# An audio tower on one core: fp16 terms for the mixture bias, causal attention with stationary values, and new order strings for every engine

## The reference, cut to what matters

```python
o = jnp.einsum('enh,ehd->end', h, W2) + b2[:, None, :]
y = jnp.einsum('ne,end->nd', comb, o)
...
scores = jnp.einsum('bhqd,bhkd->bhqk', q, k) * dh ** (-0.5)
causal = jnp.tril(jnp.ones((n, n), bool))
scores = jnp.where(causal, scores, jnp.finfo(scores.dtype).min)
attn = jax.nn.softmax(scores, axis=-1)
o = jnp.einsum('bhqk,bhkd->bhqd', attn, v)
y = o.transpose(0, 2, 1, 3).reshape(b, n, d) @ Wo
gate = jax.nn.softmax(y @ gate_W + gate_b, axis=-1)
...
out = jnp.einsum('bned,bne->bnd', eo, gate)
```

## Time and profile before

| | |
|---|---|
| median of 3 runs | 4183.73 us (4181.23 to 4189.27) |
| the profiled execution | 4183.28 us |
| its span, first to last instruction | 4181.6 us |
| busy share of the span | PE 96%, DVE 78%, ACT 66%, POOL 61% |
| granted clock of TensorE, mean | 0.984 of full speed |
| one round of the 30 | 122.3 us |

### The profile page before, as it was taken

How to read it: one execution, slowest core, us unless ns; L and a number is a source line. 1 busy time by engine, 2 the same in 40 slices (tenths; PEclk the granted TensorE clock), 3 DMA queues, 4 the chain that set the end, 5 groups by cost and what they waited for, 6 DMA issues and landing times.

```text
span 4181.6 us, 104776 instructions
## 1 busy us (share of the span) xinstructions
PE 3994.9 (96%) x41344; PEld 3003.6 (72%) x41344; DVE 3258.6 (78%) x8879; ACT 2767.7 (66%) x4797; POOL 2531.2 (61%) x2494
## 2 busy tenths in 40 slices
PE   9589999999999999999999999999999999999988
PEld 4256777777777777777777777777777777777766
DVE  4367887878888777888878888878878887887866
ACT  4236776766767666677776767776676777667654
POOL 2136666666666666666666666666666666666656
PEclk9679999999999999999999999999999999999999
DMA  6100100010110000111000011100111110010100
GB/s 184 40 28 29 31 27 23 16 31 29 31 31 27 21 20 29 31 31 31 19 22 26 29 31 31 31 19 18 30 29 31 31 31 19 17 31 29 29 16 7
DMA packets 137083, 127.62 MB, mean 31 GB/s; under 512 B 28944, under 2 KB 135376, under 8 KB 136592
## 3 DMA queue, kind: packets, MB, share of 16 engines
q1 hardware_dynamic: 136592, 120.91, 9.9%
HBM read 71.05 MB, written 49.55 MB: 29 GB/s over the span
## 4 chain that ended last, share of the span: by engine, by line
PE 80%; DVE 7%; ACT 6%; issue 3%; DMA 2%; SPq 1%; POOL 1%; ACTq 0%; DVEq 0%; POOLq 0%
PE pf L1313 14%; PE pf L1315 13%; PE pf L1314 13%; PE pa L1574 8%; PE pa L1313 4%; PE pa L1315 4%; PE pa L1314 4%; PE pa L1359 3%; PE pa L1460 3%; PE pa L1556 3%; PE pa L1422 2%; PE pa L1446 2%; PE pa L1654 2%; DVE h L1297 2%; ACT hid L902 2%
## 5 line engine op out<-in xcount | busy, mean ns | idle before, releaser
L680 POOL TENSOR_TENSOR hid_lo<-hid,hid_hi 128x504 f16<-128x504 f32 x1536 | 1793.0, 1177 | 1132.3 <-DVE hid_hi L1278 1132.2
L902 ACT ACTIVATE hid<-pf,vec 128x504 f32<-128x504 f32 x1536 | 1017.2, 679 | 469.7 <-PE pf L1315 377.1
L1313 PE MATMUL pf<-w_hi,hid_hi 128*126 128x128 f16 x6144 | 1129.5, 223 | 9.4 <-DVE h L1297 6.5
L1315 PE MATMUL pf<-w_hi,hid_lo 128*126 128x128 f16 x6144 | 1115.0, 221 | 0.0
L1314 PE MATMUL pf<-w_lo,hid_hi 128*126 128x128 f16 x6144 | 1114.7, 221 | 0.0
L1313 PEld LDWEIGHTS pf<-w_hi,hid_hi 128*126 128x126 f16 x6144 | 843.2, 137 | 136.4 <-DVE h L1297 60.7
L1314 PEld LDWEIGHTS pf<-w_lo,hid_hi 128*126 128x126 f16 x6144 | 844.4, 137 | 31.1
L1315 PEld LDWEIGHTS pf<-w_hi,hid_lo 128*126 128x126 f16 x6144 | 845.8, 138 | 0.0
L1278 DVE CAST hid_hi<-hid 128x504 f16<-128x504 f32 x1536 | 774.3, 523 | 35.2 <-ACT hid L902 26.6
L1297 DVE SCALAR_TENSOR_TENSOR h<-pf,gates,h 126x128 f32<-126x128 f32 x2048 | 572.9, 341 | 112.3 <-PE pf L1315 109.4
L1313 PE MATMUL pf<-xf_hi,w_hi 128*128 128x504 f16 x1536 | 581.8, 379 | 21.6 <-ACT hid L902 20.3
(11 more groups left out here) (208 smaller groups left out, 7401.7 us busy)
## 6 DMA issues: line engine op xcount, KB each, us to landing
qk_spread<-terms SPq DMA_DIRECT2D x224, 126.0 KB, 2.5
qk_spread<-terms SPq DMA_DIRECT2D x192, 63.0 KB, 2.3
y_scratch<-hid SPq DMA_DIRECT2D x32, 252.0 KB, 2.1
y_in<-y_scratch SPq DMA_DIRECT2D x32, 252.0 KB, 3.2
terms<-qk_hi SPq DMA_DIRECT2D x32, 252.0 KB, 2.4
terms<-qk_lo SPq DMA_DIRECT2D x32, 252.0 KB, 2.4
qk_spread<-terms SPq DMA_DIRECT2D x32, 252.0 KB
terms<-ot_hi SPq DMA_DIRECT2D x32, 252.0 KB, 2.4
```

Source lines behind the costliest of these rows:

```text
L680: nc.gpsimd.tensor_tensor(hid_lo[:, c % 8], hid[:, c % HIDS], hid_hi[:, c % 8], ALU.subtract).then_inc(hid_lo_done[c % 2], 1)
L902: nc.scalar.activation(hid[:, c % HIDS], pf[:, c % 2, 0:TOK], func, bias=vec[:, bias:bias + 1]).then_inc(F["hid_ready"], 1)
L1313: nc.tensor.matmul(out, ah, bh, start=start, stop=False, skip_group_check=skip)
L1315: return nc.tensor.matmul(out, al, bh, start=False, stop=stop, skip_group_check=skip)
```

## The change

1. **Mixture bias in fp16.** After the gates are made, DVE writes them as 96 fp16 columns: the rounded gates twice and the rest once (`split_gates`, two instructions, twice a pair). `b2` is loaded three times over (12 DMAs in place of 4) and POOL splits it once (`split_bias2`, two instructions, at pair 0). The transpose becomes one fp16 matmul with an identity, and each of the four fp32 matmuls an fp16 one. PE no longer waits for `b2` ahead of its first transpose, but ahead of the first bias product.
2. **Causal attention with stationary values.** The values (64 columns of a head) become the stationary operand and the turned probabilities the moving one, with 252 columns for the first key tile and 126 for the second; head 0 writes PSUM partitions 0 to 63, head 1 partitions 64 to 127. The result comes out turned, so that the last four transposes go. Since tokens now lie along the columns, the division moves ahead of the turn: DVE scales the probabilities by the inverse row sums (two reciprocals and eight `tensor_scalar`, once a pair), and PE's turn of the probabilities waits for it (`p2_scaled`). ACT may copy the third and fourth turned block only when the first sequence's products are done.
3. **Finer steps.** Bare yields go, and long steps are cut: the projections of q, k and v, the four tiles of values and of `qkv2`, the two halves of `qk2turn`, statistics and their aggregation, each exponential, each band product and others are steps of their own. Engines take only the chunk steps in which they do something (`each` has a filter).
4. **New order strings** for all engines. The count of work in a round is the same.

```diff
-def each(work, chunks):
+def each(work, chunks, takes):
     for chunk in chunks:
-        work(*chunk)
-        yield
+        if takes(*chunk):
+            work(*chunk)
+            yield
...
+BIAS_TERMS = 3
...
-            for i in range(TILES):
-                sp.dma_start(b2[i * EXPERTS:(i + 1) * EXPERTS, :, i], b2_dram).then_inc(small_loaded, 16)
+            for term in range(BIAS_TERMS):
+                for i in range(TILES):
+                    first = (term * TILES + i) * EXPERTS
+                    sp.dma_start(b2[first:first + EXPERTS, :, i], b2_dram).then_inc(small_loaded, 16)
...
+            def split_bias2():
+                pool.wait_ge(small_loaded, 32 + 16 * TILES * BIAS_TERMS)
+                nc.gpsimd.tensor_copy(b2_terms[:], b2[:]).then_inc(b2_split, 1)
+                pool.wait_ge(b2_split, 1)
+                low = slice(TILES * EXPERTS, 2 * TILES * EXPERTS)
+                nc.gpsimd.tensor_tensor(b2_terms[low], b2[low], b2_terms[low], ALU.subtract).then_inc(b2_split, 1)
...
+            def split_gates(a, p):
+                S = SS[a]
+                dve.wait_ge(S["gate_made"], n(p + 1))
+                nc.vector.tensor_copy(gate_terms[0:TILE, a, 0:64].rearrange("p (s c) -> p s c", s=2),
+                                      gates_all[0:TILE, a].unsqueeze(1).to_broadcast([TILE, 2, TILES * EXPERTS])
+                                      ).then_inc(S["gate_hi"], 1)
+                dve.wait_ge(S["gate_hi"], n(p + 1))
+                nc.vector.tensor_tensor(gate_terms[0:TILE, a, 64:96], gates_all[0:TILE, a], gate_terms[0:TILE, a, 0:32],
+                                        ALU.subtract).then_inc(S["gate_ready"], 1)
...
-                dve.wait_ge(S1["pv2_done"], n(p * 4 + 4))
-                nc.vector.reciprocal(inv_sum[0:TILE], row_sum[0:TILE].rearrange("p t h -> p (t h)")
-                                     ).then_inc(S1["rs_rec"], 1)
-                dve.wait_ge(S1["rs_rec"], n(p + 1))
-                nc.vector.tensor_tensor(
-                    xn[1][0:TILE].rearrange("p t (h d) -> p (t h) d", d=HEAD2),
-                    pa1[0:TILE, 1].rearrange("p (c d) -> p c d", d=HEAD2),
-                    inv_sum[0:TILE].unsqueeze(2).to_broadcast([TILE, 8, HEAD2]), ALU.mult
-                ).then_inc(S1["o2_ready"], 1)
+                for b in range(2):
+                    dve.wait_ge(S1["p2_ready"], n(p * 4 + 2 * b + 2))
+                    nc.vector.reciprocal(inv_sum[0:TILE, 4 * b:4 * b + 4],
+                                         row_sum[0:TILE, 2 * b:2 * b + 2].rearrange("p t h -> p (t h)")
+                                         ).then_inc(S1["rs_rec"], 1)
+                    dve.wait_ge(S1["rs_rec"], n(p * 2 + b + 1))
+                    for hd in range(HEADS2):
+                        i = 2 * b + hd
+                        for qt, c in halves:
+                            at = 4 * b + 2 * qt + hd
+                            last = nc.vector.tensor_scalar(p2[i][0:TILE, c], p2[i][0:TILE, c],
+                                                           inv_sum[0:TILE, at:at + 1], None, ALU.mult)
+                        last.then_inc(S1["p2_scaled"], 1)
+                    yield
...
             pe.wait_ge(w_lo_done, PIECES)
-            pe.wait_ge(small_loaded, 32 + 16 * TILES)
+            pe.wait_ge(small_loaded, 32)
...
-                nc.tensor.transpose(pa[a][:, GATES_T[a], 0:TILE], gates_all[0:TILE, a],
-                                    ident[0:TILE, 0:TILE]).then_inc(SS[a]["gate_turned"], 1)
+                nc.tensor.matmul(pa[a][:, GATES_T[a], 0:TILE], gate_terms[0:TILE, a], ident16[0:TILE, 0:TILE],
+                                 start=True, stop=True).then_inc(SS[a]["gate_turned"], 1)
...
-                    last = nc.tensor.matmul(pa[a][0:TILE, BIAS2[a], i * D:(i + 1) * D], gate_t[a][:], b2[:, a, i],
-                                            start=True, stop=True)
+                    last = nc.tensor.matmul(pa[a][0:TILE, BIAS2[a], i * D:(i + 1) * D], gate_t[a][:],
+                                            b2_terms[:, a, i], start=True, stop=True)
...
-                            for m, (kt, blk) in enumerate(blocks):
-                                last = nc.tensor.matmul(pa1[0:TILE, 1, first:first + HEAD2],
-                                                        fs1[0:TILE, j % 2, cols(blk)],
-                                                        qkv[0:TILE, 2 * b + kt, c0:c0 + HEAD2], start=(m == 0),
-                                                        stop=(m == len(blocks) - 1))
-                        last.then_inc(S1["pv2_done"], 1)
-                    yield
-                pe.wait_ge(S1["o2_ready"], n(p + 1))
-                turn(1, p * 7 + 6, xn[1])
+                def causal_values(b):
+                    pe.wait_ge(S1["p2t_ready"], n(p * 4 + 2 * b + 2))
+                    for kt, first, width in ((0, 0, SEQ), (1, TILE, TILE)):
+                        for hd in range(HEADS2):
+                            c0 = 2 * D + hd * HEAD2
+                            last = nc.tensor.matmul(pa1[head_rows(hd), TURN, b * SEQ + first:b * SEQ + first + width],
+                                                    qkv[0:TILE, 2 * b + kt, c0:c0 + HEAD2],
+                                                    fs1[0:TILE, hd, kt * SEQ:kt * SEQ + width], start=(kt == 0),
+                                                    stop=(kt == 1), skip_group_check=True)
+                    last.then_inc(S1["turned"] if b else S1["pv2_done"], 1)
...
-PE_ROUND = ("llhhoahhaohaolohallhooloqholahhoahoahoalhhalholahloalaolalhoalloalhallaqaolahlahlhaolahloolhhqll"
+PE_ROUND = ("hhaoohoaohhlaohllhaolohhlaohlhaolaoaohhaaaolahlhalllooallaaalllhallhaallloollhhallaaaloaloahlalh"
```

More of the change, by code:

```diff
@@ L32 @@
 BAND, BAND_WIDTH = 5, 131
-POOL_EVEN = True
 HIDS = 4
@@ L222, in each, with every_chunk, no_chunk, last_of_expert @@
     for chunk in chunks:
-        work(*chunk)
-        yield
+        if takes(*chunk):
+            work(*chunk)
+            yield
+def every_chunk(kind, p, c):
+    return True
+def no_chunk(kind, p, c):
+    return False
+def last_of_expert(kind, p, c):
+    per = (CHUNKS0, CHUNKS1)[kind]
+    return c % per == per - 1
+def last_of_pair(kind, p, c):
+    return kind == 1 and c == EXPERTS * CHUNKS1 - 1
 def in_order(order, parts):
@@ L1660, in linear_and_causal_attention, with turn_probabilities @@
-                pe.wait_ge(S1["o2_ready"], n(p + 1))
-                turn(1, p * 7 + 6, xn[1])
+                def turn_probabilities(i):
+                    if i:
+                        pe.wait_ge(S1["p2t_ready"], n(p * 4 + i))
+                    else:
+                        pe.wait_ge(S1["s2_masked"], n(p * 4 + 4))
+                    pe.wait_ge(S1["p2_scaled"], n(p * 4 + i + 1))
+                    for blk in range(3):
+                        last = nc.tensor.transpose(pa1[0:TILE, 0, cols(blk)], p2[i][0:TILE, cols(blk)],
+                                                   ident[0:TILE, 0:TILE])
+                    last.then_inc(S1["p2_turned"], 1)
```

479 lines of the change are left out of this document (205 added, 274 removed).

## The result

| | before | after |
|---|---|---|
| median | 4183.35 us (4181.23 to 4189.27) | 4127.64 us (4125.44 to 4132.9) |
| ratio, 95% interval | | 0.9866, 0.9849 to 0.9884 |
| span of the profiled execution | 4181.6 us | 4123.7 us |

The account below looks back on a forecast made before the run. PE was taken to bound the rounds; 122.35 us less 2.7 of work and 1.5 of waits gave 118.1, DVE's stretch 118.4. 118 us over 30 rounds plus 8 at start and end gave 4057 us, range 4000 to 4108.

Parts of the forecast that it names:

- The work taken off PE: Bias, turn of the gates and causal values on PE: 2.7 us a round less, giving 119.6 with the old waits.
- rival 1: Products in halves don't overlap (1.1 a round), or old waits return elsewhere (1.5): round 119.6, 4092 us; chance 0.2.
- The drain: Tiling-mode change around the causal products in halves empties PE: 0.17 us each way, 0.7 a pair, round 119.1; not adopted.
- The waits: PE's four largest waits, for ACT's copies, a gelu and the turned maxima: 1.5 us a round less, giving 118.1.
- DVE's stretch: DVE from the sum of squares, 80.4 us into the round, to the last gated sum: 39.6 us, giving round 118.4.
- Rival 3: DVE's eight scalings each lose 1 us beside POOL: stretch 47.5, round 126.3, kernel 4295 us; chance 0.05.
- Rival 2: Every PE wait goes, if DVE's stretch is 38.3: round 117.1, kernel 4014 us; chance 0.13.
- Start and end: Outside the 30 rounds: 5 us saved at the start, 3 at the end; new strings could shift some 5.
- Costs that I set at nothing: The output's store in its new place and ACT's added table loads: neither expected to lengthen the round.
- The output's store: Now ahead of the softmax query and key loads: costed at nothing, at most 0.8 us a round.
- ACT's table loads: Two more a round at 1283 ns on ACT: covered by PE's work and costing nothing, 2.6 us if uncovered.

Follow-up runs that it names:

- the extra work early: The changed kernel with two more 252-column tensor_scalar on DVE, results unused, at the first half's logits, 78 us into a round: 4132.98 us.
- the gelu first: The changed kernel with DVE's logits ahead of the cast of chunk (0,0) and ACT's copy of the turned gates behind the gelu of chunk (0,5): 4113.63 us.
- the one with the waits covered: DVE and ACT orders of the run with the squares first; on PE chunk (0,6) goes ahead of the gates' turn, (0,7) between it and the bias: 4103.6 us.
- the run with the squares first: The gelu first, plus DVE's sum of squares (L1220) ahead of the last steps of the gates' softmax: 4107.69 us.
- the run with the top 2 first: The one with the logits first, plus DVE's choice of the top 2 and gate split ahead of the sum of squares: 4179.73 us.
- the one with the logits first: The changed kernel with DVE's logits of the softmax half ahead of the cast of chunk (0,0): 4114.65 us.

## Why the prediction was wrong

**The work taken off PE: right in its pieces, wrong in its sum.** A bias product in fp16 holds PE for 0.06 us. The eight records of the new values are these, with what follows them:

```profile
2023.30 0.86 PE L1642 MATMUL pa<-fs,v 126*64 126x252 f32 x8
2024.09 0.27 PE L1312 MATMUL pf<-w_hi,hid_hi 128*126 128x128 f16 x1
```

That is 0.79 us a visit against 0.74 forecast; one after the other they would have needed 1.28. So the halves run side by side, and the first half of rival 1 falls. The drain of the Trainium skill, TensorEngine Tiling (Array Packing), Key Properties, by which I had 0.17 each way, would have made it 1.08; the row shows 0.05 beyond my sum.

But PE's busy time fell by 1.6 us a round, where the sum was 2.7. I split the round by kinds of product, from start to next start without the idle time. The bias and the turn of the gates take 1.3 less (forecast 1.4), the causal values and the last turn 1.2 less (forecast 1.4), and all other products together take 1.0 more. Half of that is in the softmax scores. Other products I had put at nothing, though the new order gives nearly every one of them new neighbours. This term is 1.1 of the 2.2 us by which the round is longer than forecast; no run tried it by itself.

**The waits: the old ones better than forecast, the new ones not foreseen.** I let 1.5 of 2.5 us go. All the four went, the gelu's too, and another of 4.9 us in total; only the turn of the probabilities still waits, 0.4 a round, now for DVE's scaling. With the new ones PE's idle time fell by 0.2 us a round, where the forecast, with 0.3 more for DVE, had 1.2. This is the other 1.0 of the 2.2.

**DVE's stretch: right in its length and its end, by luck in part.** From the sum of squares to the last gated sum it takes 39.05 us in every round (forecast 39.6), and it ends 1.63 us into the next round (forecast 1.7 with 0.1 behind it).

```profile
2120.72:2159.77 39.05, 36.37 (x118) 1.00 0.14 42
2145.93 1.13 DVE L1296 SCALAR_TENSOR_TENSOR h<-pf,gates,h 126x128 f32<-126x128 f32 x4 [1.20 <-PE pf L1314]
```

The forecast was 38.3 busy "if DVE never waits". DVE is busy 36.4, and waits 1.8 in the stretch, 1.2 of it for PE at 108 us. And PE has no wait ahead of the first `o` chunk of a round, where the forecast let DVE hold it. DVE holds PE from 82 to 105 us (and by 0.2 at 117), and PE holds DVE at 108.

**DVE's stretch: wrong in its start, and this is the step that failed.** The forecast put L1220 at 80.4 us into the round: "PE has 0.7 us more in front of it now, and fewer waits: 80.4". It begins at 83.2 on average (82.6 to 84.4). With 39.05 - 1.63 behind it that is the round, 120.6. This sum holds by definition; what it says is that L1220 is 2.8 us late and the shorter stretch gives 0.6 of it back. It is the same 2.2 us as above, seen from DVE. A round of the short kind, 120.03 us from 2759.84, shows its parts:

```profile
2839.90 1.13 DVE L1296 SCALAR_TENSOR_TENSOR h<-pf,gates,h 126x128 f32<-126x128 f32 x4 [0.26 <-PE pf L1314]
2841.36 1.17 DVE L1011 TENSOR_TENSOR lg<-lge,lmax 126x32 f32<-126x32 f32 x1
2842.45 1.21 DVE L1220 TENSOR_REDUCE ss<-o 126x16 f32<-126x1024 f32 x1
```

- PE has the product for this gated sum ready at 80.05 us. L1220 at 80.4, with the 1.1 us of the gated sum ahead of it, would have needed it at 79.3. PE is 0.75 late; in before it came at 79.6.
- The last operations of the gates' softmax now stand between the gated sum and L1220, 0.5 us. I took this 0.5 off the stretch and didn't add it in front.
- L1011, the last of them, runs beside POOL and takes 1.17 where it needs 0.19: 1.0.

These make 2.2, so that L1220 begins at 82.6. In the other kind of round the casts of (0,0) and (0,1) take 1.39 and 2.16 where 0.41 does. The gated sum then begins at 81.5, held up by DVE's own work, and L1011 is quick: 0.4 more than in the short kind. The rest of the average, 0.3, comes from the rounds in which PE has waited at 26 us for a DMA; before has such rounds as well.

So in the short rounds DVE came free in time for the gated sum, by 0.26 us where before had 1.83, and what I left out is behind this point. The gated sum stands just ahead of the stretch of the earlier trace rows, which is where I began to read.

That DVE's order at this place sets the round is shown by the runs: exchanges of a few letters on it gave between -0.75 and +1.9 us a round (the -0.75 holds a letter of ACT's, which gave nothing by itself), extra work there costs and elsewhere doesn't, and filling PE's waits gave 0.01. Where one operation grew or shrank by a meeting with POOL, the round followed in full or in part: +0.5 for the scaled queries in one run, -0.4 of 0.9 for L1011 in another. A run without any meeting wasn't tried, nor one that takes away PE's 0.75, so that the three terms are read from the trace and not tested one by one.

**Rival 3: right mechanism, wrong victims.** The scalings take 277 to 353 ns, all of them; none is held up by POOL. Two casts and L1011 were, some 20 us ahead of where I looked. I had priced this by the casts' mean, 519 ns; over the whole program it is 539 now. A mean of 48 casts a round hides two that stand on the path.

**Rival 2** (all waits gone, 117.1) had the old waits right, but neither the new ones that came in their place nor PE's 1.1 us.

**Start and end: 5 and 3 forecast, 12.5 and -8.0 measured.** Both go with the clock. What the clock lacks to 1, times the length, is at most what is lost at the lower of the two levels (exactly that, if PE's work sets the pace all along): of the end 0.08 x 157.7 = 12.6 us after, 0.03 x 149.7 = 4.5 before, a difference of 8.1. Three slices of 10 us of after's end, in their order. In the first PE is busy 7.18 of 10 at a clock of 0.99. In the second the clock is 0.67, a mixture of the two levels, and in the third 0.51, the lower level, 1.2 GHz, nearly throughout; PE is busy 9 of 10 in both and the other engines are mostly idle. In the slice between these two, left out here, the clock is 1.00 again:

```profile
3983.70:3993.70 10.00, 7.18 (x64) 4.48 (x62) 2.55 (x7) 4.84 (x8) 3.75 (x4) 0.99 0.29 77
3993.70:4003.70 10.00, 9.26 (x65) 8.51 (x66) 4.24 (x12) 1.16 (x2) 2.15 (x2) 0.67 0.01 2
4013.70:4023.70 10.00, 8.74 (x52) 8.58 (x53) 2.73 (x9) 0.55 (x1) 1.14 (x1) 0.51 0.01 2
```

The ends of two of the runs above, the extra work early and the gelu first. Their orders of the end are after's, letter for letter:

```profile
3973.50:4128.00 154.50, 130.30 (x1265) 96.80 (x1263) 93.41 (x234) 69.19 (x119) 81.62 (x70) 0.94 0.05 13
```

```profile
3956.40:4118.00 161.60, 138.05 (x1274) 104.57 (x1272) 94.11 (x235) 69.12 (x119) 82.24 (x71) 0.89 0.04 12
```

They differ by 7 us, with five hundredths of clock between them. In the start the clock went from 0.83 to 0.85, and 0.17 x 361.5 - 0.15 x 349 = 9 us of the 12.5 go with it. The wait of 7.83 us for `b2` is gone as well, but 6.21 for DVE stand in its place, and PE's first product of the second phase begins at 132.65, 1.8 us earlier. The fp16 bias alone has this too, and its start was 7 us longer than before's.

**Costs that I set at nothing.** The output's store in its new place: PE's waits for the spread terms are 8.2 us over the rounds, 0.3 a round, within the 0.8 that I gave as the bound; in before they were 5.9. ACT's table loads: the gelu of (0,0) is late by one, and the cast of (0,0) waits 0.99 for it. That it is in both kernels doesn't make it free: it stands at the head of the stretch in which DVE is short. The softmax scores' 0.5 I had not seen. PE comes to them eight times a round in both kernels; in after four of these visits are 0.04 to 0.23 us longer, in every round the same ones. Why these four, the runs don't show.

## What to carry to other kernels

When PE sheds work at a place where another engine just keeps up with it, ask for the other engine's slack there, not for its share of the round: here DVE had 1.8 us before one operation at 80 us, and this place, not its 19% of idle time, told where it would become late. A stretch of work that one prices right must also start when one thinks, so its head needs the same accounting as its body: an operation that is moved out of the stretch is still in front of it. And where two engines exclude each other, price the pairs that the new order puts side by side on the critical stretch, by name, since the mean over the round says nothing of them. Last, a sum of what goes off an engine isn't what it is busy less when all else on it is put in a new order as well: here 2.7 became 1.6.

Of the versions tried, the one with the waits covered is the fastest that computes everything: 4103.6 us, 0.9799 of before, against 0.9866 for the change. It differs from the change by a few letters in three strings, and the run with the squares first (4107.69) has the same round.

## What was not expected of the hardware

The order is worth more than the operations. Two neighbouring letters of DVE's order, 1.3 us of its work put later, cost 2.2 us a round (the run with the top 2 first against the one with the logits first), by a wait for POOL and a meeting with it; a short move on PE cost 1.4. The new causal part is worth 4.4 us a round in the orders made for it; the new bias is worth 0.7 in the new orders and 0.26 in the old, for 1.3 of work.

With one order of the end, that end took 154.5 to 162.0 us in the runs above, with mean clocks from 0.94 to 0.89, while two rounds of nearly the same order agree to 0.02 (120.24 and 120.26). A median that differs by 5 us says little here; the round does.
